# Mixture-of-experts stages: down projection as split matmuls with the weights stationary, experts summed in PSUM, activations weighted by routing weights that a DMA spreads over the partitions

## The reference, cut to what matters

```python
def _L0_ffn_ref(x, router_W, router_b, sW1, sb1, sW2, sb2, eW1, eb1, eW2, eb2):
    shared = relu(xt @ sW1 + sb1) @ sW2 + sb2
    probs = softmax(xt @ router_W + router_b)            # 15 experts
    top_p, top_i = top_k(probs, 3)
    cw = zeros((n, 15)).at[arange(n)[:, None], top_i].set(top_p)
    h = relu(einsum('nd,edh->neh', xt, eW1) + eb1)       # all experts, 128 -> 128
    ye = einsum('neh,ehd->ned', h, eW2) + eb2            # 128 -> 128
    routed = einsum('ned,ne->nd', ye, cw)
    return shared + routed
x = x + _L0_ffn_ref(_layernorm(x), ...)
```

## Time and profile before

| what | us |
|---|---|
| median of three runs (2197.45 to 2200.65) | 2197.6 |
| span of the profiled execution | 2195.9 |
| ffn1a, from its first DVE instruction to its last | 231.7 |
| PE busy in the span | 1937.5 (88%) |
| DVE busy in the span | 1695.5 (77%) |
| ACT busy in the span | 1035.0 (47%) |
| POOL busy in the span | 492.2 (22%) |

### The profile page before, as it was taken

One profiled execution on the slowest core, in us unless ns is written; L12 is line 12 of the kernel. 1 busy time (PEld: TensorE's weight loads), 2 busy tenths in 40 slices (PEclk: granted clock), 3 DMA queues, 4 the chain that ended last, 5 costly groups with the idle time before them and its releaser, 6 DMA issues. The chain is left out here.

```text
span 2195.9 us, 35701 instructions
## 1 busy us (share of the span) xinstructions
PE 1937.5 (88%) x12178; PEld 1438.1 (65%) x12178; DVE 1695.5 (77%) x5509; ACT 1035.0 (47%) x1617; POOL 492.2 (22%) x558
## 2 busy tenths in 40 slices
PE   5886799998999967673799979999999999989999
PEld 3554699986899923332799965555555555549998
DVE  6997788876888879998688877766767767738887
ACT  3442244433444434442444444666666665554443
POOL 1110100012000022230200024534544543330000
PEclk8998999999999988876899989999999999999999
DMA  3000100000000010000000000000000000000000
GB/s 100 6 5 4 56 1 1 1 1 1 1 1 1 1 40 1 0 1 0 1 1 1 1 1 1 1 1 1 1 1 1 1 1 1 1 1 11 11 9 13
DMA packets 17638, 15.73 MB, mean 7 GB/s; under 512 B 4209, under 2 KB 16177, under 8 KB 16946
## 3 DMA queue, kind: packets, MB, share of 16 engines
q1 hardware_dynamic: 15152, 12.66, 1.8%
q10 hardware_dynamic: 2306, 0.78, 0.2%
HBM read 10.55 MB, written 2.88 MB: 6 GB/s over the span
## 5 line engine op out<-in xcount | busy, mean ns | idle before, releaser
L2205 ACT ACTIVATE soft_prob<-psum 128x1024 f32<-128x1024 f32 (+3 forms) x384 | 302.4, 812 | 203.8 <-PE psum L2085 202.2
L2297 DVE TENSOR_REDUCE soft_mx<-psum 128x1 f32<-128x512 f32 (+2 forms) x352 | 231.0, 688 | 116.1 <-PE psum L2155 79.3
L2155 PE MATMUL psum<-soft_own,soft_stack 128*128 128x512 f32 (+3 forms) x768 | 249.3, 376 | 24.5 <-DVE soft_mx L2293 10.7
L163 POOL TENSOR_TENSOR norm_rstd<-norm_mv,s_const_minus_half 128x4 f32<-128x4 f32 x64 | 65.2, 1019 | 915.0 <-DVE norm_mv L158 908.4
L2085 PE MATMUL psum<-soft_stack,soft_own 128*128 128x512 f32 (+3 forms) x768 | 225.4, 377 | 2.8 <-POOL soft_stack L2062 2.2
L2085 PEld LDWEIGHTS psum<-soft_stack,soft_own 128*128 128x128 f32 x768 | 125.3, 189 | 133.2 <-issue 81.6
L2293 DVE CUSTOM_DVE_ANT_0 psum<-psum,s_soft_sel 128x384 f32<-128x384 f32 (+1 forms) x256 | 157.4, 639 | 64.8 <-PE psum L2155 64.0
L2155 PEld LDWEIGHTS psum<-soft_own,soft_stack 128*128 128x128 f32 x768 | 139.8, 193 | 92.7 <-DVE soft_mx L2297 42.9
L1075 DVE SCALAR_TENSOR_TENSOR x<-psum,ffn1b_cw,x 128x128 f32<-128x128 f32 x512 | 144.1, 344 | 29.7 <-PE psum L949 20.9
L2102 PE MATMUL psum<-soft_prob,soft_v_pad 128*32 128x512 f32 (+3 forms) x1536 | 163.6, 498 | 3.5 <-ACT soft_prob L2205 2.1
L1075 DVE SCALAR_TENSOR_TENSOR x<-psum,ffn1a_cw,x 128x128 f32<-128x128 f32 x512 | 144.2, 344 | 27.2 <-PE psum L949 18.1
(11 more groups left out here) (381 smaller groups left out, 4114.0 us busy)
## 6 DMA issues: line engine op xcount, KB each, us to landing
s_ffn_w<-in_ffn_w SPq DMA_DIRECT2D x4, 1024.0 KB, 7.8
out_x<-x SPq DMA_DIRECT2D x8, 256.0 KB, 2.3
x<-in_x SPq DMA_DIRECT2D x4, 384.0 KB, 8.0
mamba_coef_dram<-mamba_out_coef SPq DMA_DIRECT2D x8, 96.0 KB, 1.6
s_ret_w<-in_ret_w SPq DMA_DIRECT2D x1, 640.0 KB, 3.5
x<-in_x SPq DMA_DIRECT2D x4, 128.0 KB, 3.5
s_ret_cos<-in_ret_cos SPq DMA_DIRECT2D x1, 512.0 KB, 7.0
s_ret_sin<-in_ret_sin SPq DMA_DIRECT2D x1, 512.0 KB, 7.3
```

The source lines that it names most:

```text
L163: self.nc.gpsimd.tensor_tensor(self.rstd[:, :], self.mv[:, :, 1], self.const["minus_half"][:, 0:GT], ALU.pow).then_inc(self.rstd_ready, 1)
L2155: ins = pe.matmul(per_head[:, n, :], stack[:, u % HT, i * P:(i + 1) * P], own[:, u % 3, g, half * BLK:half * BLK + width], start=(n == 0), ...
L2205: nc.scalar.activation(prob[:, done % PROBS, :, low(n):BLK], e_ps[:, n % 2, :, low(n):BLK], ACT.Exp, scale=float(HD) ** -0.5).then_inc(exp ...
L2297: nc.vector.tensor_reduce(mx[:, i, half, heads.start:heads.stop], bank[:, 0:width * len(heads)].rearrange("p (g k) -> p g k", k=width), AX ...
```

## The change

The down projection changes sides: w2 (again as high and low F32R halves, `w2_high`, `w2_low`) becomes the stationary operand and h the moving one, 512 tokens at a time, so that the result has channels on the partitions (`yt_ps`). All 16 experts and the bias of a block add up in one PSUM bank. So the weight of a token must be in h before the matmul: DVE `weigh` computes t = (h_ps + b1) * cw from PSUM, where the token's weight must stand on every partition. ACT `halves` then writes relu(t) twice, once as F32R (`h_high`) and once in place in full; `low_h`, on POOL for three experts in four and on DVE for the fourth, writes the difference as `h_low`. PE `down` runs three F32R matmuls of 512 columns. At the end of a block ACT copies the sum (`copy_y`), PE transposes it back (`transpose_y`) and DVE adds it to x (`add`), once a block. The weights get to all partitions by DMA: `copy_cwt` also writes them as rows, SP stores the 16 rows to DRAM and loads them back in four chunks of four experts (8 KB on each of 128 partitions, the last one 6 KB), in a ring of six chunks. PE's order is now one `up` and one `down` a step, four steps apart (`LAG`); `up` has three banks. In ffn0a the fetch of later weights moves from the stage's start to its second block.

```diff
+FULL = slice(B2_ROWS, B2_ROWS + NE)
+H_BANKS, T_RING, H_RING, LAG = 3, 4, 4, 4
+CHUNK_E = 4
+CHUNKS_E = NE // CHUNK_E
+CW_RING = 6
...
+            def broadcast_weights(q):
+                sp.wait_ge(cwt_ready, q + 1)
+                if q >= 2:
+                    sp.wait_ge(t_ready, NE * (q - 1) - 1)
+                sp.dma_start(cw_dram[q % 2, :, :], cw_rows[FULL, q % 2, :]).then_inc(cw_stored, 16)
+                sp.wait_ge(cw_stored, 16 * (q + 1))
+                for c in range(CHUNKS_E):
+                    k = CHUNKS_E * q + c
+                    if k >= CW_RING:
+                        old_q, old_c = divmod(k - CW_RING, CHUNKS_E)
+                        sp.wait_ge(t_ready, NE * old_q + CHUNK_E * old_c + chunk_experts(old_c))
+                    experts = slice(CHUNK_E * c, CHUNK_E * c + chunk_experts(c))
+                    sp.dma_start(cw_all[:, k % CW_RING, 0:chunk_experts(c), :],
+                                 cw_dram[q % 2, experts, :].unsqueeze(0).to_broadcast([P, chunk_experts(c), BLK]))\
+                        .then_inc(cw_loaded[k % CW_RING], 16)
...
+            broadcast_weights(0)
             for g in range(BLOCKS):
+                if g == 1 and fetch is not None:
+                    for dst, src in fetch[0]:
+                        sp.dma_start(dst, src).then_inc(fetch[1], 16)
+                if out is not None and g:
+                    store_x(g - 1)
+                if g + 1 < BLOCKS:
+                    broadcast_weights(g + 1)
...
+            def low_h(n):
+                pool.wait_ge(full_ready, n + 1)
+                if n >= H_RING:
+                    pool.wait_ge(down_done, n - H_RING + 1)
+                nc.gpsimd.tensor_tensor(h_low[:, n % H_RING, :], t[:, n % T_RING, :], h_high[:, n % H_RING, :],
+                                        ALU.subtract).then_inc(low_pool, 1)
...
+            for g in range(BLOCKS):
+                for e in range(NE):
+                    if e == 0 and (more or out is None):
+                        norm.invert(pool, g + 1)
+                    if not on_dve(n):
+                        low_h(n)
+                    if e == 2 and more:
+                        split_x(g + 1, (g + 1) % 2)
...
+            def up(n):
+                if n >= H_BANKS:
+                    pe.wait_ge(t_ready, n - H_BANKS + 1)
...
+            def down(n):
+                g, e = divmod(n, NE)
+                y = yt_ps[:, g % 2, :]
+                if e == 0:
+                    pe.wait_ge(cwt_ready, g + 1)
...
+                    pe.matmul(y, b2_parts[:, :], cwt[0:B2_ROWS, g % 2, :], start=True, stop=False)
...
+                pe.wait_ge(high_ready, n + 1)
+                pe.matmul(y, w2_high[:, e, :], h_high[:, n % H_RING, :], start=False, stop=False)
+                pe.matmul(y, w2_low[:, e, :], h_high[:, n % H_RING, :], start=False, stop=False)
+                pe.wait_ge(*lows(n))
+                pe.matmul(y, w2_high[:, e, :], h_low[:, n % H_RING, :], start=False, stop=e == NE - 1)\
+                    .then_inc(down_done, 1)
...
+            for n in range(H_BANKS):
+                up(n)
+            transpose_cw(0, 0)
+            for n in range(H_BANKS, STEPS_ALL + LAG):
+                g, e = divmod(n, NE)
+                if n < STEPS_ALL:
+                    up(n)
+                    if e == 3 and (g + 1 < BLOCKS or out is None):
                         norm.transpose(pe, g + 1)
+                    if e == 5 and g + 1 < BLOCKS:
+                        route(g + 1, (g + 1) % 2)
+                    if e == 10 and g + 1 < BLOCKS:
+                        transpose_cw(g + 1, (g + 1) % 2)
+                    if e == 6 and g:
+                        transpose_y(g - 1)
+                if n >= LAG:
+                    down(n - LAG)
+            transpose_y(BLOCKS - 1)
...
+            def halves(n):
+                act.wait_ge(t_ready, n + 1)
+                if n >= H_RING:
+                    act.wait_ge(down_done, n - H_RING + 1)
+                    act.wait_ge(*lows(n - H_RING))
+                nc.scalar.activation(h_high[:, n % H_RING, :], t[:, n % T_RING, :], ACT.Relu).then_inc(high_ready, 1)
+                nc.scalar.activation(t[:, n % T_RING, :], t[:, n % T_RING, :], ACT.Relu).then_inc(full_ready, 1)
...
+            for n in range(STEPS_ALL):
+                halves(n)
+                if e == 1 and (g + 1 < BLOCKS):
+                    copy_x(g + 1, (g + 1) % 2)
...
+                if e == 2 and g:
+                    copy_y(g - 1)
+                if e == 4 and g + 1 < BLOCKS:
+                    exp(g + 1)
+                if e == 8 and g + 1 < BLOCKS:
+                    copy_cwt(g + 1, (g + 1) % 2)
+            copy_y(BLOCKS - 1)
...
+            def weigh(n):
+                dve.wait_ge(h_ready, n + 1)
+                if n >= T_RING:
+                    dve.wait_ge(*lows(n - T_RING))
...
+                if i == 0:
+                    dve.wait_ge(cw_loaded[k % CW_RING], 16 * (k // CW_RING + 1))
+                nc.vector.scalar_tensor_tensor(t[:, n % T_RING, :], h_ps[:, n % H_BANKS, :], w["b1"][:, e:e + 1],
+                                               cw_all[:, k % CW_RING, i, :], ALU.add, ALU.mult).then_inc(t_ready, 1)
...
+            for n in range(STEPS_ALL):
+                weigh(n)
+                if n >= 2 and on_dve(n - 2):
+                    low_h(n - 2)
+                if e == 0 and (more or out is None):
+                    norm.statistics(dve, g + 1)
+                if e == 1 and (more or out is None):
+                    norm.scale(dve, g + 1)
+                if e == 4 and more:
+                    shift(g + 1)
+                if e == 5 and g:
+                    add(g - 1)
+                if e == 6 and more:
+                    probabilities(g + 1)
+                if e == 7 and more:
+                    largest(g + 1)
+                if e == 8 and more:
+                    combine_weights(g + 1, (g + 1) % 2)
+            low_h(STEPS_ALL - 1)
+            add(BLOCKS - 1)
```

More of the change, by code:

```diff
@@ L848, in ffn_stage @@
         xt_high, xt_split = sem("xt_high"), sem("xt_split")
-        W1_PIECES = (0, 4, 8, NE)
-        block = ctx.enter_context(nc.Block())
-        def blocks(body):
-            for g in range(BLOCKS):
-                body(g, g % 2, g < BLOCKS - 1)
-        if fetch is not None:
-            @block.sync
-            def _(sp):
-                for dst, src in fetch[0]:
-                    sp.dma_start(dst, src).then_inc(fetch[1], 16)
-        if out is not None:
-            stored = sem("stored")
-            @block.sync
-            def _(sp):
-                for g in range(BLOCKS):
-                    sp.wait_ge(acc_done, NE * (g + 1) + Y_BANKS - 1)
-                    rows = slice(g * GT, (g + 1) * GT)
-                    sp.dma_start(out[:, rows, :], x[:, rows, :]).then_inc(stored, 16)
+        STEPS_ALL = NE * BLOCKS
@@ L941, in down @@
                     pe.wait_ge(cwt_ready, g + 1)
-                    if split:
+                    if g >= 2:
+                        pe.wait_ge(yt_copied, g - 1)
+                    if split and g == 0:
                         pe.wait_ge(b2_ready, 1)
-                for j in range(GT):
-                    if e == E:
-                        pe.matmul(y_ps[:, e % Y_BANKS, j, :], cwt[:, p, j * P:(j + 1) * P], b2_parts[:, :],
-                                  start=(j == 0), stop=False, skip_group_check=True)
@@ L1079, in body @@
-            def body(g, p, more):
-                if more or out is None:
-                    norm.statistics(dve, g + 1)
-                    norm.scale(dve, g + 1)
-                dve.wait_ge(cw_ready, g + 1)
-                for e in range(NE):
-                    add_expert(g, p, e)
-                    if more and e == 7:
-                        shift(g + 1)
-                    if more and e == 9:
-                        probabilities(g + 1)
-                    if more and e == 11:
-                        largest(g + 1)
-                    if more and e == 13:
-                        combine_weights(g + 1, 1 - p)
+                nc.vector.tensor_tensor(low, whole, high, ALU.subtract).then_inc(cw_ready, 1)
```

225 lines of the change are left out of this document (117 added, 108 removed).

## The result

The changed kernel takes 2275.6 us (median of four runs, 2270.8 to 2277.5) against 2197.8 for the kernel before on the same chip: ratio 1.0347, 95% interval 1.0333 to 1.0362. The forecast was 2187.1 with a range up to 2240, so it missed both the sign and the range. The profiled execution took 2270.8, its span of 2269.1 is 73.2 us longer than before, and the four mixture stages hold nearly all of it: ffn0a 253.0 instead of 231.7, ffn0b 243.4 instead of 229.9, ffn1a 251.7 instead of 231.7, ffn1b 248.1 instead of 230.7, each from its first DVE instruction to the end of the last one that adds to x. That is 72.4 together.

What follows compares the result with a forecast made beforehand. PE was taken as the bound, busy 139.67 of 140.00 us. A block of 24.85 + 0.9 + 0.5 = 26.25 us, with stage starts and ends, saves 10.5 over four stages: 2197.6 - 10.5 = 2187.1 us, range 2150 to 2240.

Steps and rivals of the forecast that it cites:

- PE's own work, 24.85: PE's instructions in one block of a mixture stage, 16 steps of 1.39 plus the rest: 24.85 us if PE never waits.
- First wait, 0.9: PE before the transposes of x, after up(3): there at 4.9, DVE's scale done at 5.8, so 0.9 us a block.
- Second wait, 0.5: PE before the transposes of cw, after up(10): there at 17.6, DVE's routing chain done at 18.1, so 0.5 us a block.
- Start, 16.4: Start of ffn1a: the first weigh comes 16.4 us after the stage's start, where the first weighted sum stood at 14.1.
- The spread weights: Routing weights through DRAM to all partitions: chunk 0 lands at 26.5, before the next block's first weigh needs it at 27.15.
- a sign that it is wrong: In the profile after: the forecast is wrong if, among other signs, a DMA ends waits of DVE inside the stages.
- The cover of chunk 0: Time between the landing of a block's first weight chunk and the weigh that wants it: 0.6 to 0.7 us.
- the late chunk: Rival, slower: chunk 0 lands beyond its 0.65 us of cover, each further microsecond costing one per block; 2249 at 200 GB/s; chance 0.16.
- DVE's middle becomes the bound: Rival, slower: DVE's list from the logits to low_h(7) runs longer, adding to the second wait; 0.8 a block, 2212; chance 0.24.
- PE doesn't wait: Rival, faster: DVE reaches scale and combine_weights sooner, both PE waits go, a block is 24.85, time 2142; chance 0.17.
- Before, the same norm stood at the head of DVE's block with a whole block's `down` queued in front of it: Part of the first wait's argument: the kernel before had a whole block's down queued there; now the norm has two steps.

Runs made afterwards that it cites:

- e1: Changed kernel with one wait added: POOL begins low_h of a block's first expert only after DVE's scale for the next block; 2200.2 us, ratio 1.0001.
- e3: Changed kernel with routing weights stored and spread only once a stage, other blocks using the first block's weights; 2275.3 us, ratio 1.0337.
- e11: Changed kernel with e5's waits, PE's transposes of x and cw a step later, SP's store earlier, down five steps behind, longer rings; 2149.1 us, ratio 0.9758.
- e4: Kernel before, with two POOL subtracts of 1.29 us that nobody reads added after each invert of the norm; 2293.5 us, ratio 1.0421.
- e5: Changed kernel with e1's wait, and POOL's last two weight splits held until after the first combine_weights; 2185.8 us, ratio 0.9930.
- e9: Changed kernel with each low_h of POOL written as two subtracts of 256 columns instead of one of 512; 2271.9 us, ratio 1.0318.
- e10: Changed kernel with PE's transposes of x and cw one step later and SP's store after the first cw copy, POOL's order unchanged; 2233.4 us, ratio 1.0145.

## Why the prediction was wrong

- *PE's own work, 24.85*: right, a little high. F32R matmuls start 0.227 apart in the kernel after, for 0.232. 26.2 less the two waits of e1 (0.6 and 1.0) leaves 24.6.
- *First wait, 0.9*: this is the step that failed. It put "`scale` 1.12" behind POOL's invert, from the earlier trace rows, where POOL has nothing to do after the invert. The same part counts 12 `low_h` of 1.29 us for POOL and puts none of them beside `scale`. They stand exactly there: POOL's list has `low_h` of experts 0 and 1 behind the invert. So 1.12 became 3.04 and the wait 2.5, and the clock fell to 0.50 behind ten of the 27 waits of the later blocks, for which the forecast had no term. With `low_h` held back the wait is 0.6.
- *Second wait, 0.5*: 1.0, after as in e1 (1.22 from start to start, less 0.227). It was put at half its length; e1's two waits together, 1.6 for 1.4, are within the 0.4 either way that the forecast allowed for a block.
- *Start, 16.4*: the chain is right (16.0 and 15.0 once POOL is out of the way), the durations of the routing chain were again taken from rows without POOL beside them: 20.7. The trace of the kernel before held a sign of it: in ffn1a this subtract with both operands in SBUF took 0.55, where its like takes 0.22, and ended 0.07 after POOL's split of weights (1054.30 to 1055.57):

```profile
1055.09 0.55 DVE L1038 TENSOR_TENSOR ffn1a_prob<-ffn1a_prob,ffn1a_top 128x60 f32<-128x60 f32 x1
```

- *The spread weights*: right but for three of the 28 inner borders. The store took 1.6 us, three times 2.0 to 2.8; chunk 0 took 4.2 to 5.0 from issue to landing and once 6.1. DVE waited for a DMA three times inside the stages, 3.7 us together, which the forecast had named as a sign that it is wrong; the time is unchanged without them (e3). The cover of chunk 0, put at 0.65, is mostly 0.5 to 1.1 in e1. So the late chunk did not happen as the rival had it, at every border. The Trainium skill's 6.15 us for a megabyte (DMA: Bandwidth & Descriptors, section Measured) is of DMAs that GpSimd issues, while SP issues these; by the trace only one of the 32 first chunks came near it.
- *Rivals*: "DVE's middle becomes the bound" came nearest by its sign; it asks for DVE's list to be longer, and even names POOL's 1.29 in front of a `weigh`, but sees the place in the second wait, with 0.8 a block. It was the first, with 1.6 and the clock. "PE doesn't wait" came near only in e11, with 25.0 for its 24.85.
- *"Before, the same norm stood at the head of DVE's block with a whole block's `down` queued in front of it"*: wrong too, by e4. There was no cover in the kernel before either; what protected it was that POOL was idle.

The four stages were to take 10.5 us less than before; in e5 they take 15.6 less (ffn0a 227.8, ffn0b 226.6, ffn1a 227.8, ffn1b 226.2). That its 2185.8 is so near the forecast 2187.1 is in part luck: the kernel before was 5 us slower beside it, and in a block 24.6, 0.6 and 1.0 stand where the forecast had 24.85, 0.9 and 0.5, with errors that cancel. What did not cancel is one kind of term: durations of DVE, read where POOL was idle, and used where the change keeps POOL busy.

## What to carry to other kernels

When a change gives POOL long instructions, list which DVE instructions will run beside them and whether their durations were read with POOL idle; here those with both operands in SBUF, and a scaling and a cast within SBUF, lasted as long as POOL's. Where such a step is on the way to the bounding engine, order POOL's list around it, which here cost one wait and gave 75 us; cutting POOL's work into pieces gave nothing clear of the noise (e9), and covering the wait, with two other moves, gave 42 (e10). A wait on PE can cost more than itself: behind ten of the 27 the clock fell, and in e4 a block with such a fall took 1.6 us longer than one without.
